# A two-layer perceiver on one core: value products of both attention passes regrouped into longer runs

## The reference

```python
def _L0_xattn_ref(x, context, Wq, Wk, Wv, Wo, bo):        # H = 8, D = 64
    q = (x @ Wq).reshape(B, Nq, H, D)
    k = (context @ Wk).reshape(B, Nkv, H, D)
    v = (context @ Wv).reshape(B, Nkv, H, D)
    sim = jnp.einsum('bihd,bjhd->bhij', q, k) * SCALE
    attn = jax.nn.softmax(sim, axis=-1)
    out = jnp.einsum('bhij,bjhd->bihd', attn, v).reshape(B, Nq, H * D)
    return out @ Wo + bo
...
x = x + _L0_xattn_ref(_layernorm(x, axis=-1), ctx_768, ...)
x = x + _L0_attn_ref(...)
x = x + _L0_ffn_ref(...)
x = x + _L1_xattn_ref(_layernorm(x, axis=-1), ctx_768, ctx_768, ...)   # 16 heads of 16
x = x + _L1_attn_ref(...)
x = x + _L1_ffn_ref(...)
```

## Time and profile before

| | |
|---|---|
| median of 3 runs | 1183.14 us (1183.11 to 1183.75) |
| profiled execution, its own time | 1184.72 us |
| its span, first to last instruction | 1182.9 us |
| mean granted TensorE clock | 0.992 of full speed |
| TensorE busy | 1138.1 us, 96% of the span |
| weight loads (PEld) busy | 928.4 us, 78% |
| DVE busy | 667.2 us, 56% |
| ACT busy | 671.1 us, 57% |
| POOL busy | 212.4 us, 18% |
| first layer's second pass | about 126 to 573 us |
| second layer's second pass | about 894 to 1106 us |

### The profile page before, as it was taken

How to read it: one execution, slowest core, us unless ns; L and a number is a source line. 1 busy time by engine, 2 the same in 40 slices (tenths; PEclk the granted TensorE clock), 3 DMA queues, 4 the chain that set the end, 5 groups by cost and what they waited for, 6 DMA issues and landing times.

```text
span 1182.9 us, 28888 instructions
## 1 busy us (share of the span) xinstructions
PE 1138.1 (96%) x10032; PEld 928.4 (78%) x10032; DVE 667.2 (56%) x1133; ACT 671.1 (57%) x1097; POOL 212.4 (18%) x312
## 2 busy tenths in 40 slices
PE   6999899999999999999887999999999999999998
PEld 4788688888888888888764888888878888888774
DVE  5999544434444443443654888888885444444442
ACT  1888343344344434433221688888888889889520
POOL 0000100000000000000002677777750110000310
PEclk9999999999999999999999999999999999999999
DMA  3445611110011001000544577767667895555370
GB/s 128 134 142 138 275 46 27 27 35 27 27 33 29 27 27 35 27 27 27 200 161 169 174 230 234 229 216 231 230 211 245 283 304 182 186 185 184 136 295 6
DMA packets 63258, 163.42 MB, mean 138 GB/s; under 512 B 6848, under 2 KB 8320, under 8 KB 57536
## 3 DMA queue, kind: packets, MB, share of 16 engines
q1 hardware_dynamic: 54592, 119.06, 30.6%
q0 software_dynamic: 8640, 44.00, 10.3%
HBM read 124.21 MB, written 38.80 MB: 138 GB/s over the span
## 4 chain that ended last, share of the span: by engine, by line
PE 82%; DVE 9%; issue 6%; ACT 1%; DVEq 1%; DMA 0%; SPq 0%; ACTq 0%
PE ps L679 55%; PE ps L927 8%; PE ps L863 8%; PE ps L714 2%; DVE wide L1376 1%; PE ps L667 1%; DVE wide L1381 1%; PE ps L725 1%; PE ps L729 1%; PE ps L726 1%; PE ps L727 1%; PE ps L728 1%; PE ps L1064 1%; PE ps L1227 1%; PE ps L1205 1%
## 5 line engine op out<-in xcount | busy, mean ns | idle before, releaser
L1444 DVE TENSOR_TENSOR wide<-wide,probs 128x1024 f32<-128x1024 f32 x97 | 118.8, 1225 | 244.5 <-ACT probs L527 244.4
L538 ACT ACTIVATE probs<-ps 128x1024 f32<-128x1024 f32 x196 | 190.1, 1024 | 23.6 <-PE ps L679 23.4
L1376 DVE TENSOR_TENSOR wide<-ps,wide 128x512 f32<-128x512 f32 (+1 forms) x196 | 187.0, 954 | 28.9 <-PE ps L679 24.5
L510 ACT CAST wide<-ps 128x512 bf16<-128x512 f32 x294 | 161.9, 586 | 31.8 <-PE ps L679 26.6
L527 ACT ACTIVATE probs<-ps 128x512 f32<-128x512 f32 x196 | 117.3, 598 | 107.2 <-PE ps L679 107.2
L679 PE MATMUL ps<-q_ha,t_ha 128*128 128x512 f32 x392 | 156.3, 399 | 4.0 <-DVE q_le L1304 3.8
L1381 DVE TENSOR_TENSOR wide<-wide 128x512 bf16<-128x512 bf16 (+1 forms) x196 | 109.2, 557 | 13.1 <-ACT wide L510 2.7
L679 PE MATMUL ps<-q_ab,q_hk 128*128 128x512 f32 x392 | 107.6, 395 | 1.4 <-DVE q_ab L1316 1.3
L927 PE MATMUL ps<-probs,v_sb 128*32 128x128 f32 x3136 | 105.9, 276 | 0.1
L1432 DVE COPY v_sb<-wide 128x256 f32<-128x256 f32 x98 | 29.0, 296 | 118.4 <-PE ps L927 117.0
L679 PEld LDWEIGHTS ps<-q_ha,t_ha 128*128 128x128 f32 x392 | 75.0, 191 | 21.8 <-DVE q_le L1304 4.3
(11 more groups left out here) (391 smaller groups left out, 2301.5 us busy)
## 6 DMA issues: line engine op xcount, KB each, us to landing
raw<-ctx_in SPq DMA_DIRECT2D x147, 256.0 KB, 2.7
k_mem<-q_hk SPq DMA_DIRECT2D x49, 512.0 KB, 3.0
v_mem<-probs SPq DMA_DIRECT2D x49, 256.0 KB, 3.3
wide<-v_mem SPq DMA_DIRECT2D x49, 256.0 KB, 4.2
ring<-ex_in POOLq DMA_DIRECT2D x8, 1152.0 KB, 11.3
q_le<-k_mem SPq DMA_DIRECT2D x17, 512.0 KB, 4.4
q_ab<-k_mem SPq DMA_DIRECT2D x16, 512.0 KB, 4.5
q_hk<-k_mem SPq DMA_DIRECT2D x16, 512.0 KB, 4.4
```

The costliest lines, as they stand in the source:

```text
L510: act.copy(half16[:, c:c + 512], ps[:, back_bank(layer, q) + u, :]).then_inc(sem(f"half{layer}"), 1)
L538: act.activation(probs[:, at:at + 1024], ps[:, bank:bank + 2, :].rearrange("p b n -> p (b n)"), ACT.Exp).then_inc(sem("exp1"), 1)
L1376: dve.tensor_tensor(r, ps[:, b:b + half // 512, :].rearrange("p b n -> p (b n)"), r, ALU.max)\
L1444: dve.tensor_tensor(run[:, 0:1024], run[:, 0:1024], e, ALU.add).then_inc(sem("lsum"), 1)
```

## The change

In the first layer, `front` takes each tile whole, its values and then its scores. `back` now issues the products of one tile. TensorE goes by fours: two fronts (four tiles), then the products of four tiles, one tile late, so that the fourth tile's products open the next run. ACT's exps0 follows: the copy of a tile's values, then its two exponentials.

In the second layer, TensorE goes in rounds of three half tiles: scores of three, then products of the three before them. The exponentials have six places, four in probs and two in scr (part of the tile named wide). In DVE's body the repetition of the next group's key rows stands ahead of both value copies of the present group.

```diff
--- before.py
+++ after.py
@@ -198,6 +198,7 @@
         e_keep = [probs[:, i * 1024:(i + 1) * 1024] for i in range(2 * GT)]
 
         stage = probs[:, 0:2048]
+        e_half = [probs[:, i * 1024:(i + 1) * 1024] for i in range(4)] + [scr[:, i * 1024:(i + 1) * 1024] for i in range(2)]
         v_in = [run[:, i * 512:(i + 1) * 512] for i in range(KSLOTS)]
         q_all = probs[:, 2048:3072]
         block = stack.enter_context(nc.Block())
@@ -250,9 +251,11 @@
                     body(i, slot, False)
             body(GROUPS // KSLOTS, 0, False, True)
 
-        def pair_bank(slot, j, w):
-
-            return s_pair[(4 * slot + 2 * j + w) % 3]
+        HALVES = 4 * KSLOTS
+
+        def pair_bank(m):
+
+            return s_pair[m % 3]
 
...
@@ -518,8 +521,6 @@
                     if not first:
                         act.wait_ge(sem("pv0"), (t - 3) * units)
                     act.copy(v_keep[GT * slot + j], ps[:, v_bank[j], :]).then_inc(sem("v_sb0"), 1)
-                for j in range(GT):
-                    t = g * GT + j
                     if not first:
                         act.wait_ge(sem("lsum"), t - 3)
                     for u in range(units):
@@ -527,16 +528,15 @@
                         act.activation(e_keep[GT * slot + j][:, u * 512:(u + 1) * 512], ps[:, s_bank[j][u], :],
                                        ACT.Exp).then_inc(sem("exp0"), 1)
 
-            def exps1(t, slot, j, first):
-
-                for w in range(2):
-                    n = 2 * t + w
-                    act.wait_ge(sem("s2_1"), n + 1)
-                    if not first:
-                        act.wait_ge(sem("pv1"), n - 3)
-                    at, bank = j * 2048 + w * 1024, pair_bank(slot, j, w)
-                    act.activation(probs[:, at:at + 1024], ps[:, bank:bank + 2, :].rearrange("p b n -> p (b n)"),
-                                   ACT.Exp).then_inc(sem("exp1"), 1)
+            def exps1(i, m, first):
+
+                n = HALVES * i + m
+                act.wait_ge(sem("s2_1"), n + 1)
+                if not (first and m < 6):
+                    act.wait_ge(sem("pv1"), n - 5)
+                bank = pair_bank(m)
+                act.activation(e_half[m % 6], ps[:, bank:bank + 2, :].rearrange("p b n -> p (b n)"),
+                               ACT.Exp).then_inc(sem("exp1"), 1)
 
...
@@ -599,8 +599,8 @@
                 act.wait_ge(sem("v_out1"), kv_count(1, GROUPS - 2))
 
                 def body(i, slot, first, last=False):
-                    for j in range(GT):
-                        exps1((KSLOTS * i + slot) * GT + j, slot, j, first and slot == 0)
+                    for m in range(4 * slot, 4 * slot + 4):
+                        exps1(i, m, first)
                 rounds(act, body)
 
...
@@ -871,83 +871,93 @@
                     pe.wait_ge(sem("split0"), g + 1)
                     for j in range(GT):
                         values(g * GT + j, j, slot, skip)
-                    for j in range(GT):
                         for u in range(units2):
                             scores2(g * GT + j, j, slot, u, skip)
 
-                def back(g, slot, start=False, stop=False):
-
-                    for j in range(GT):
-                        for u in range(units2):
-                            products(g * GT + j, j, slot, u, start and j == 0, stop and j == GT - 1)
-
-                def step(g, slot, first):
-
-                    front(g + 1, 1 - slot)
-                    back(g, slot, first and slot == 0)
+                def back(t, j, slot, start=False, stop=False):
+
+                    for u in range(units2):
+                        products(t, j, slot, u, start, stop)
+
+                def four(i, first):
+
+                    front(2 * i, 0, first)
+                    front(2 * i + 1, 1)
+                    if not first:
+                        back(4 * i - 1, 1, 1)
+                    back(4 * i, 0, 0, first)
+                    back(4 * i + 1, 1, 0)
+                    back(4 * i + 2, 0, 1)
 
                 def second0():
 
                     keep_warm(4, 5)
-                    front(0, 0, True)
-                    step(0, 0, True)
-                    step(1, 1, True)
+                    four(0, True)
                     with pe.Fori(1, GROUPS // 2) as i:
-                        step(2 * i, 0, False)
-                        step(2 * i + 1, 1, False)
-                    back(GROUPS - 1, 0, stop=True)
-
-                def pairs1(i, slot, j, new=False):
-
-                    if j == 0:
-                        if new and slot == 0:
+                        four(i, False)
+                    front(GROUPS - 1, 0)
+                    back(TILES - 3, 1, 1)
+                    back(TILES - 2, 0, 0)
+                    back(TILES - 1, 1, 0, stop=True)
+
+                def scores_half(i, m, new=False):
+
+                    slot, j, w = m // 4, m // 2 % 2, m % 2
+                    if m % 4 == 0:
+                        if new and m == 0:
                             pe.wait_ge(sem("q_hi"), 3)
                         else:
                             pe.wait_ge(sem("k_again"), KSLOTS * i + slot)
-                    t = (KSLOTS * i + slot) * GT + j
-                    for w in range(2):
-                        n = 2 * t + w
-                        if not (new and n < 3):
-                            pe.wait_ge(sem("exp1"), n - 2)
-                        bank = pair_bank(slot, j, w)
-                        for u in range(4 * w, 4 * w + 4):
-                            last = mm(ps[:, bank + u % 4 // 2, (u % 2) * 256:(u % 2 + 1) * 256],
-                                      kp[slot][:, u * GK + j * P:u * GK + (j + 1) * P], q_ha[:, u * 256:(u + 1) * 256], 0, 1)
-                        last.then_inc(sem("s2_1"), 1)
-
-                def products1(t, j, start, stop):
-
-                    for w in range(2):
-                        pe.wait_ge(sem("exp1"), 2 * t + w + 1)
-                        if w == 0:
-                            pe.wait_ge(sem("v_sb1"), t + 1)
-                        for u in (2 * w, 2 * w + 1):
-                            for k in range(4):
-                                h = 4 * u + k
-                                last = pe.matmul(ps[32 * k:32 * k + 32, 4, u * P:(u + 1) * P],
-                                                 v_sb[j][:, h * 32:(h + 1) * 32],
-                                                 probs[:, j * 2048 + h * P:j * 2048 + (h + 1) * P],
-                                                 start=(start and u == 0), stop=stop, skip_group_check=True)
-                        last.then_inc(sem("pv1"), 1)
+                    if not (new and m < 3):
+                        pe.wait_ge(sem("exp1"), HALVES * i + m - 2)
+                    bank = pair_bank(m)
+                    for u in range(4 * w, 4 * w + 4):
+                        last = mm(ps[:, bank + u % 4 // 2, (u % 2) * 256:(u % 2 + 1) * 256],
+                                  kp[slot][:, u * GK + j * P:u * GK + (j + 1) * P], q_ha[:, u * 256:(u + 1) * 256], 0, 1)
+                    last.then_inc(sem("s2_1"), 1)
+
+                def products_half(i, m, start=False, stop=False):
+
+                    j, w = m // 2 % 2, m % 2
+                    pe.wait_ge(sem("exp1"), HALVES * i + m + 1)
+                    if w == 0:
+                        pe.wait_ge(sem("v_sb1"), HALVES // 2 * i + m // 2 + 1)
+                    for u in (2 * w, 2 * w + 1):
+                        for k in range(4):
+                            h = 4 * u + k
+                            at = (h - 8 * w) * P
+                            last = pe.matmul(ps[32 * k:32 * k + 32, 4, u * P:(u + 1) * P], v_sb[j][:, h * 32:(h + 1) * 32],
+                                             e_half[m % 6][:, at:at + P], start=(start and u == 0), stop=stop,
+                                             skip_group_check=True)
+                    last.then_inc(sem("pv1"), 1)
 
                 def second1():
 
                     keep_warm(12, 3)
                     pe.wait_ge(sem("q_lo"), 2)
                     pe.wait_ge(sem("max_row"), 32)
-                    pairs1(0, 0, 0, True)
-
-                    def body(i, slot, first, last=False):
-                        t = (KSLOTS * i + slot) * GT
-                        pairs1(i, slot, 1, first)
-                        products1(t, 0, first and slot == 0, False)
-                        if not last:
-                            if slot < KSLOTS - 1:
-                                pairs1(i, slot + 1, 0, first)
-                            else:
-                                pairs1(i + 1, 0, 0)
-                        products1(t + 1, 1, False, last)
-                    rounds(pe, body)
+                    def threes(i, new=False):
+
+                        for q in range(HALVES // 3):
+                            for m in range(3 * q, 3 * q + 3):
+                                scores_half(i, m, new)
```

(19 more changed lines are left out.)

## The result

| | before | after |
|---|---|---|
| median, first comparison | 1183.45 us (1183.11 to 1185.41) | 1166.03 us (1163.65 to 1168.80) |
| ratio, 95% interval | | 0.9843 (0.9827 to 0.9859) |
| profiled execution, its span | 1184.72, 1182.9 us | 1163.65, 1161.9 us |
| TensorE busy | 1138.1 us | 1116.8 us |
| first layer's pass, first to last product | 141.45 to 569.77 us | 138.69 to 559.19 us |

The forecast was 1165.0 us within 1162.5 to 1170, faster. It holds: 17.4 us less, where the sum said 18.2.

The account below looks back on a forecast made before the run. TensorE, never resting in either layer's second pass, was taken as the bound. Terms 7.8 + 0.3 + 10.2 - 0.45 + 0.28 = 18.2 us off a median of 1183.1 gave 1165 us, range 1162.5 to 1170.

Parts of the forecast that it names:

- The turn in the first layer: First layer's second pass: 23 trips from scores to products and back go, at 0.341 us each, gaining 7.8 us.
- Rival (d): The 0.34 us is paid where products wait for values or exponentials, so only start and tail move: 1183 us; chance 0.03.
- The tail: End of first layer's pass: tile 96's scores come 1.16 us earlier, against 0.87 more products ahead; gain 0.3 us.
- Cover for the fourth tile's values and the splits: First layer, ACT: later value copies delay the split's end to 6.0 us, needed at 10.8; cover 4.8, cost nothing.
- The turn in the second layer: Second layer's second pass: 31 trips from scores to products and back go, at 0.33 us each, gaining 10.2 us.
- the start: Start of second layer's pass: scores wait for exponentials and first products start at 898.0 with none done; 0.45 us lost.
- the end: End of second layer's pass: four halves of products together cover the wait for the last exponential; 0.28 us gained.
- DVE's order, cost nothing, with keys due in 6.1 us: Second layer: key repetition ahead of value copies costs nothing if keys land within 6.1 us; q_le loads take 5.5, later 4.1.
- the 7.1 for the other phases: Second layer: in the other phases scores need the repetition first, and keys may take 7.1 us to land.
- Rival (a): Second layer, first 36 tiles: loads become the bound, 17 groups keep their old pace, 3.6 us, 1168.6 us; chance 0.12.
- Rival (b): Second layer: TensorE is bound by instruction issue, a round keeps 3.24 us, kernel takes 1175 us; chance 0.07.
- Rival (c): Second layer: key repetition first makes a serial ring; keys landing at 7.2 us throughout eat 18.2 us; chance 0.02.

Follow-up runs that it names:

- l0_only: Only the first layer's part of the change, second layer as in the kernel before: 1176.97 us, ratio 0.9929 to the kernel before.
- l1_only: Only the second layer's part of the change, first layer as in the kernel before: 1174.41 us, ratio 0.9925 to the kernel before.
- loads_half: The changed kernel with POOL's weight loads released one per four value copies instead of every two: 1166.78 us, ratio 0.9850 to the kernel before.

## Why the prediction was right, step by step

- **The turn in the first layer**, 23 x 0.341 = 7.8 us: shown. 7.83 from first to last product in l0_only, and the price again from 71 turns added, 8 more taken away, and its vanishing with the shape. Rival (d) falls.
- **The tail**, 0.3: right. From the last product to the end of DVE's last sum are 3.37 us in the kernel before and in l1_only, and 3.01 us in the change and in l0_only: 0.36.
- **Cover for the fourth tile's values and the splits**, cost nothing: right. PE has no gap inside or ahead of a run, though ACT's copies of these tiles stood waiting for products, 23 times and up to 3.9 us. The split ended at 320.69, 5.8 us behind the last score matmul at 314.90; 6.0 was forecast, and it is needed at 10.8. ACT's waits:

```profile
ACT weights_q L523 <- PE ps L863: 90.0, 23, 3.9
```

- **The turn in the second layer**, 31 x 0.33 = 10.2, with -0.45 for the start and +0.28 for the end, 10.03 net: 10.50 in loads_half, which has no long round (211.09 - 200.59). The term was a little small: over thirty rounds one takes 3.067 on average, 3.24 - 3.067 is half a turn, so a turn is 0.347 and 31 of them 10.75. Start and end together then cost 0.25, where the sum had 0.17. No run tests them apart, but their rows do show it: the first products start 3.58 us behind the first exponential (898.0 - 894.51 = 3.49 in the sum), so with the 0.87 of the first two halves' products the kernel is at 4.45 where it was at 3.90 before, and the start cost 0.55 and not 0.45; the last two halves' products start 0.73 apart before and 0.44 in the change, 0.29 for the end.
- **DVE's order, cost nothing, with keys due in 6.1 us**: here the step missed. The limit was right: in three profiles of the change the loads of q_le that took 6.96, 6.86, 6.78, 6.51, 6.47 and 6.27 us to land made rounds 0.93, 0.83, 0.72, 0.55, 0.42 and 0.22 us too long, and a load of q_hk that took 6.81 cost nothing, as the 7.1 for the other phases said. What was wrong is that these loads would land as before. In the kernel before no load of q_le in this pass took over 5.87 us (the 5.5 of the earlier trace rows is the median of two) and none of any keys over 6.1, so even the worst old landing was covered. The change also moves POOL: its loads, one every 4.3 us before, now come in threes, 3.5, 3.5 and 5.3 us apart outside the long rounds, because the value copies that release them are no longer evenly spaced. The third of each three is issued within 0.2 us of a load of q_le, where it was 0.6 before. Twice in the first profile both were slow: issued at 898.2 and 898.3, they landed after 7.8 and 6.86 us, and at 923.5 and 923.7 after 7.9 and 6.96. Other such meetings cost nothing, so what makes a load late is not shown. The long rounds cost 1.76, 0.97 and 0.94 us in the three profiles. Rival (a) priced all 17 groups, 3.6 us; the truth lies between.
- **Rival (b)**, issue rate: 60 records in 3.07 us are 51 ns each, less than the 54 before; a bound at 54 would have kept 3.24. **Rival (c)**, the serial ring: its place was right and its price was 1 to 2 us, not 18.
- **The sum**, 18.2: the medians give 17.4, 17.9 and 17.2 us in three comparisons, and 18.2 - 1.2 for the mean of the long rounds + 0.5 for the second layer's pass without them = 17.5. The two errors have opposite signs, which brings the sum a little closer than its terms. The 54 turns carry it, and came at 7.83 + 10.75 = 18.6 us where it had 18.0.

## What to carry to other kernels

- Where TensorE is busy all the time, take the distance between starts over one period, subtract each kind's own steps, and look for a remainder where the shape of the array changes. Here it was 0.34 us for each change there and back: group products of one shape into long runs. Each doubling of the run halves the turns that are left, and asks for more buffers.
- An instruction moved ahead of others in an engine's order takes its slowest wait along. The landing times of the old trace, the worst included, hold only for the old order of requests: here 5.87 us became 6.96. Where the cover is a few tenths, look at what the new order makes coincide.
- Count steps at the lower clock before comparing spans: one profile here looked 3 us better than the change is.

## What the runs showed of the hardware that I had not expected

- The granted clock at one place differs from execution to execution of the same program on the same load: 1.00 and 0.75 in 127 to 135 us, worth 439.13 - 436.51 = 2.6 us, with the same matmuls at the same distances ahead of both. What decides it stays open. It is about half of the 5.2 us over which the first four runs of the change spread.
- The turn costs about the same for 64 columns (0.34) as for 32 (0.35), and the length of the run doesn't change it much: 0.33 to 0.35 with runs of 16, 32, 64 and 96 records.
- At a change of shape the weight load starts together with its matmul (315.22, 318.86), and elsewhere 0.23 us ahead of a wide one; with products over 128 columns it is ahead at the change too (224.72 for 224.94).
